# Ten-table embedding kernel on Trainium2: x in 58 loads, weights in blocks of up to 16 tiles

## The reference

```python
VOCABS = [12500, 6250, 2500, 1250, 625, 250, 1000, 500, 200, 100]
embs = [jnp.dot(x, w) for x, w in zip(xs, ws)]     # x: 1024 x vocab, w: vocab x 64, float32
emb_sum = sum(embs)
q_emb   = sum(jnp.dot(x ** 2, w ** 2) for x, w in zip(xs, ws))
fm_ans  = 0.5 * (emb_sum ** 2 - q_emb)
return jnp.concatenate([fm_ans] + embs, axis=-1)
```

## Time and profile before

| | before |
|---|---|
| median of 3 runs | 276.47 us (276.41 to 276.67) |
| the profiled execution, own time | 276.46 us |
| its span, first to last instruction | 274.7 us |
| DMA: packets, bytes, rate over the span | 15710, 113.92 MB, 415 GB/s |
| busy: PE / DVE / ACT / POOL | 78% / 82% / 82% / 42% of the span |
| x loads | 42 of 2048 KB, 9 of 1024, 11 of 512, 4 of 256 |
| weight loads | 31, of 32 to 256 KB |
| granted TensorE clock, mean | 0.988 |

### The profile page before, as it was taken

How to read it: one execution, slowest core, us unless ns; L and a number is a source line. 1 busy time by engine, 2 the same in 40 slices (tenths; PEclk the granted TensorE clock), 3 DMA queues, 4 the chain that set the end, 5 groups by cost and what they waited for, 6 DMA issues and landing times.

```text
span 274.7 us, 2715 instructions
## 1 busy us (share of the span) xinstructions
PE 213.9 (78%) x891; PEld 151.0 (55%) x892; DVE 224.1 (82%) x136; ACT 224.7 (82%) x269; POOL 114.9 (42%) x82
## 2 busy tenths in 40 slices
PE   0529889699988867878887787788788688698995
PEld 0416566476756555656654555555555465466763
DVE  2676876888798798878978978987987897999985
ACT  1649998999988788899868878877877796899994
POOL 0446757585414109267235135045045051073922
PEclk9968999999999999999999999999999999999999
DMA  7999999999999999999999999999999999999997
GB/s 263 441 402 440 410 420 417 426 421 442 416 424 426 427 420 426 421 423 428 420 424 430 420 431 428 417 424 429 420 427 431 419 423 430 410 414 416 410 398 269
DMA packets 15710, 113.92 MB, mean 415 GB/s; under 512 B 2000, under 2 KB 3280, under 8 KB 9168
## 3 DMA queue, kind: packets, MB, share of 16 engines
q1 hardware_dynamic: 11088, 106.96, 92.9%
q10 hardware_dynamic: 4608, 6.79, 6.7%
HBM read 110.85 MB, written 2.88 MB: 414 GB/s over the span
## 4 chain that ended last, share of the span: by engine, by line
DMA 63%; ACT 13%; issue 12%; PE 7%; SPq 1%; POOL 1%; ACTq 1%; DVE 0%; POOLq 0%
DMA x_ring<-in_x_dram 58%; ACT is_set L379 9%; PE sums L510 6%; DMA whole<-in_w_dram 5%; ACT turned L390 2%; SPq L327 1%; ACT whole L371 1%; POOL total L481 1%; ACT results L395 1%; ACTq L365 1%; PE sums L520 0%; ACT L371 0%; PE sums L554 0%; POOL high L468 0%; PE sums L527 0%
## 5 line engine op out<-in xcount | busy, mean ns | idle before, releaser
L604 DVE TENSOR_SCALAR_CACHE_REDUCE is_one<-x_ring 128x4096 uint8<-128x4096 f32 (+2 forms) x59 | 219.6, 3732 | 45.9 <-DMA x_ring<-in_x_dram 44.4
L379 ACT ACTIVATE is_set<-x_ring 128x2048 fp32r<-128x2048 uint32 (+2 forms) x106 | 190.1, 1796 | 32.1 <-DMA x_ring<-in_x_dram 31.6
L510 PE MATMUL sums<-is_set,low 128*128 128x512 f32 x396 | 133.1, 417 | 57.8 <-ACT is_set L379 42.8
L510 PE MATMUL sums<-is_set,high 128*128 128x512 f32 x396 | 124.9, 396 | 0.0
L510 PEld LDWEIGHTS sums<-is_set,low 128*128 128x128 f32 x396 | 68.1, 190 | 97.7 <-ACT is_set L379 43.3
L468 POOL CAST high<-whole 128x1024 fp32r<-128x1024 f32 (+5 forms) x31 | 27.1, 874 | 140.9 <-ACT whole L371 140.9
L510 PEld LDWEIGHTS sums<-is_set,high 128*128 128x128 f32 x396 | 75.5, 191 | 17.5
L470 POOL TENSOR_TENSOR low<-whole,high 128x1024 fp32r<-128x1024 f32 (+5 forms) x31 | 60.8, 1961 | 2.5
L371 ACT ACTIVATE whole<-whole 128x512 f32<-128x512 f32 (+5 forms) x31 | 16.5, 535 | 7.3 <-DMA whole<-in_w_dram 7.3
L379 ACT ACTIVATION_READ_ACCUMULATOR is_set<-x_ring 128x1 f32 x106 | 19.8, 187 | 0.0
L481 POOL TENSOR_TENSOR total<-total,turned 128x1024 f32<-128x1024 f32 x8 | 19.2, 2398 | 0.0
(11 more groups left out here) (37 smaller groups left out, 13.7 us busy)
## 6 DMA issues: line engine op xcount, KB each, us to landing
x_ring<-in_x_dram SPq DMA_DIRECT2D x42, 2048.0 KB, 21.5
x_ring<-in_x_dram SPq DMA_DIRECT2D x9, 1024.0 KB, 19.1
x_ring<-in_x_dram SPq DMA_DIRECT2D x11, 512.0 KB, 17.8
whole<-in_w_dram ACTq DMA_DIRECT2D x21, 256.0 KB, 9.7
out_dram<-results SPq DMA_DIRECT2D x9, 256.0 KB, 9.1
x_ring<-in_x_dram SPq DMA_DIRECT2D x4, 256.0 KB, 14.3
whole<-in_w_dram ACTq DMA_DIRECT2D x2, 192.0 KB, 7.1
whole<-in_w_dram ACTq DMA_DIRECT2D x4, 64.0 KB, 8.8
```

The source lines that it names most:

```text
L379: nc.scalar.activation(is_set[chunk.k % SETS][:, 0:length], in_ring(chunk.place, length).bitcast(U32), ACT.Sign, accum_out=set_counts[:, c ...
L510: last = nc.tensor.matmul(sums[:, summing(n, half), :], w, x[:, at:at + HALF], start=first, stop=False, skip_group_check=True)
L604: nc.vector.tensor_scalar(is_one[c % 2][:, to:to + length], in_ring(at, length), 1.0, None, ALU.is_equal, ALU.add, accum_out=one_counts[:, ...
```

## The change

Three things change. In `ORDER`, groups of 5 tiles (`FIVE = [2, 2, 1]`) take the place of the rests: table 3 is 5 + 5 instead of 8 + 2, the end of table 1 is 4 + 5 instead of 8 + 1, the end of table 0 is 5 + 5 instead of 8 + 2. A group of five is one load of x of 2560 KB and two counts on VectorE, of 4 tiles and of 1. In the last table two single-tile chunks share one load of 2 tiles. Together: 66 loads of x become 58 (6 of 2560 KB, 36 of 2048, 11 of 1024, 1 of 512, 4 of 256), VectorE's 59 counts become 61, 106 chunks become 108. The places in the ring move: 19 tiles, loads 0 to 5, are loaded without a wait, and load 43 starts again at the head of the ring, leaving tiles 16 to 19 of it unused for that round.

Weights are loaded in blocks: block 0 is groups 0 to 2, and after it each block is two groups, up to 16 tiles, in one of two buffers. A block whose groups belong to one table is one DMA, otherwise one per table. 15 blocks make 20 DMAs. The first two blocks (five DMAs) are issued at the start; block b is issued in the group that lies two before the first group of block b-1. `square` waits until every DMA of its block has landed. The pairs of weight parts are three instead of four.

```diff
 FULL = [2, 2, 2, 2]
+FIVE = [2, 2, 1]
...
-    (4, [[2, 2, 1]]),
+    (4, [FIVE]),
     (7, [[2, 2]]),
-    (3, [FULL, [2]]),
-    (1, [FULL] * 6 + [[1]]),
+    (3, [FIVE, FIVE]),
+    (1, [FULL] * 5 + [[2, 2], FIVE]),
     (6, [FULL]),
-    (0, [FULL] * 12 + [[2]]),
+    (0, [FULL] * 11 + [FIVE, FIVE]),
...
-WHOLES = 3
-PAIRS = 4
+BLOCK = 16
+FIRST = 3
+WHOLES = 2
+PAIRS = 3
...
-        self.whole, self.pair = g % WHOLES, g % PAIRS
+        self.pair = g % PAIRS
+        self.block, self.slot = 0 if g < FIRST else (g - FIRST) // 2 + 1, 0
...
-        elif one.table == LAST:
-            parts = [(chunk.tile, chunk.n) for chunk in chunks]
         else:
             parts = [(one.tile, sum(chunk.n for chunk in chunks))]
...
+for block in BLOCKS:
+
+    block.landed = sum(len(other.parts) for other in BLOCKS[:block.b + 1] if other.whole == block.whole)
...
-            def load_w(group):
-                if group.g >= WHOLES:
-
-                    act.wait_ge(parts_ready, group.g - WHOLES + 1)
-                at, n = group.tile * D, group.tiles
-                act.dma_start(whole[group.whole][:, 0, 0:n, :], w_dram[group.table][:, at:at + n * D]
-                              ).then_inc(w_landed[group.whole], 16)
+            def load_w(block):
+                if block.b >= WHOLES:
+
+                    act.wait_ge(parts_ready, BLOCKS[block.b - WHOLES].last + 1)
+                for table, tile, n, slot in block.parts:
+                    act.dma_start(whole[block.whole][:, 0, slot:slot + n, :],
+                                  w_dram[table][:, tile * D:(tile + n) * D]).then_inc(w_landed[block.whole], 16)
 
             def square(group):
-                act.wait_ge(w_landed[group.whole], 16 * (group.g // WHOLES + 1))
-                w = whole[group.whole][:, :, 0:group.tiles, :]
+                block = BLOCKS[group.block]
+                act.wait_ge(w_landed[block.whole], 16 * block.landed)
+                w = weights_of(group)
...
-            for group in GROUPS[:AHEAD]:
-                load_w(group)
+            for block in BLOCKS[:WHOLES]:
+                load_w(block)
...
-                        if group.g + AHEAD < NGROUPS:
-                            load_w(GROUPS[group.g + AHEAD])
+                        for block in BLOCKS[WHOLES:]:
+                            if BLOCKS[block.b - 1].first - AHEAD + 1 == group.g:
+                                load_w(block)
```

More of the change, by code:

```diff
@@ L95, in __init__ @@
         self.g, self.place, self.table, self.tile = g, place, table, tile
-        self.whole, self.pair = g % WHOLES, g % PAIRS
-        self.chunks, at = [], 0
+        self.pair = g % PAIRS
+        self.block, self.slot = 0 if g < FIRST else (g - FIRST) // 2 + 1, 0
+        self.chunks, self.sizes, at = [], sizes, 0
         for n in sizes:
@@ L145, in plan_counts @@
             parts = [(one.tile, 1), (one.tile + 1, 1)]
-        elif one.table == LAST:
-            parts = [(chunk.tile, chunk.n) for chunk in chunks]
         else:
             parts = [(one.tile, sum(chunk.n for chunk in chunks))]
+        if one.group.sizes == FIVE and one.at:
+            load = counts[-1].loads[0]
+            counts.append(Count(len(counts), [load], chunks))
+            counts[-1].at, counts[-1].length = load.at + one.at * BATCH, BATCH
+            one.place, one.load, load.count = counts[-1].at, load, counts[-1]
+            continue
+        if one.group.sizes == FIVE:
+            parts = [(one.tile, sum(FIVE))]
         length = sum(n for _, n in parts) * BATCH
@@ L159, in plan_counts @@
         counts.append(Count(len(counts), own, chunks))
+        if one.group.sizes == FIVE:
+            counts[-1].length = LOAD * BATCH
         place = own[0].at
@@ L174, in plan_counts, with __init__ @@
     return loads, counts
+class Block:
+    def __init__(self, b, groups):
+        self.b, self.whole, self.first, self.last = b, b % WHOLES, groups[0].g, groups[-1].g
+        self.parts, slot = [], 0
+        for group in groups:
+            group.slot = slot
+            if self.parts and self.parts[-1][0] == group.table:
+                self.parts[-1][2] += group.tiles
+            else:
+                self.parts.append([group.table, group.tile, group.tiles, slot])
+            slot += group.tiles
+        assert slot <= BLOCK
+BLOCKS = [Block(b, [group for group in GROUPS if group.block == b]) for b in range(GROUPS[-1].block + 1)]
+for block in BLOCKS:
+    block.landed = sum(len(other.parts) for other in BLOCKS[:block.b + 1] if other.whole == block.whole)
 LOADS, COUNTS = plan_counts()
@@ L226, in rec_kernel @@
         probe_high = sb("probe_high", [P, 1], F32R)
-        whole = [sb(f"whole{i}", [P, 2, GROUP, D], F32) for i in range(WHOLES)]
+        whole = [sb(f"whole{i}", [P, 2, BLOCK, D], F32) for i in range(WHOLES)]
         high = [sb(f"high{i}", [P, GROUP, 2 * D], F32R) for i in range(PAIRS)]
@@ L283, in upper, with weights_of @@
             return words.bitcast(BF16).rearrange("p (e h) -> p e h", h=2)[:, :, 1]
+        def weights_of(group):
+            return whole[BLOCKS[group.block].whole][:, :, group.slot:group.slot + group.tiles, :]
         def part_of(group, part):
@@ L458, in _ @@
                 g = group.g
-                w, first = whole[group.whole][:, :, 0:group.tiles, :], part_of(group, high)
+                w, first = weights_of(group), part_of(group, high)
                 pool.wait_ge(squared, g + 1)
@@ L465, in _ @@
                     nc.gpsimd.tensor_copy(pieces[:, 0, :].rearrange("p (m d) -> p m d", m=2),
-                                          whole[group.whole][:, :, group.tiles - 1, :]
+                                          w[:, :, group.tiles - 1, :]
                                           ).then_inc(pieces_ready, 1)
```

## The result

The changed kernel takes 281.96 us, the median of six runs; the kernel before took 276.44 us beside it (276.35 to 276.67, six runs). Five of the six lie between 280.56 and 282.52; the sixth ran in a slow state, at a mean TensorE clock of 0.576, took 347.17 us and is left out of the ratio. The ratio is 1.0183, 95% interval [1.0165, 1.0201]. The time went up by 5.5 us by the medians and 5.1 by the ratio, where 0.7 were forecast, and it is above the range. The profiled execution took 280.82 us, 4.4 more than that of before, with a span of 279.1 where it was 274.7.

A forecast was written before the change was run, and what follows sets the result against it. The prediction took the kernel to be bound by its 16 DMA engines. Its terms, -1.4 + 1.1 + 1.0 = +0.7 on 276.46 us, gave 277.2 us, own range 276.6 to 278.6, 8-in-10 range 275.3 to 278.8.

The forecast's parts named there:

- Term 1: DMA queues: 19 loads fewer, 171 packets per engine at 8.4 ns, save 1.4 us.
- The case of a fixed time that holds the engines: All DMAs: about 2.0 us fixed per DMA would make nineteen fewer worth 38 us; chance 0.01.
- Rival (d): Loads of x: 20 KB rows are cut, so packets aren't fewer; +0.4, 277.6 us; shares the forecast's chance of 0.48.
- Term 2: Start: joint weight waits make ScalarE late and leave DMA engines idle at 40 to 60 us; +1.1 us, bounds 0 to 2.5.
- the catching up: ScalarE, 6.5 us late near 26 us, regains 2.5 from waits it no longer has, staying 4.0 late at 53.5.
- Where the fifth weight load lands: Start: the fifth weight load lands with the fifth load of x, 14 tiles in, at 22.7 us.
- Term 3: End: the last table's tiles 16 and 17 share one load, so TensorE finishes later; +1.0 us, ends 0 and 1.3.
- sign (4): End, in the new profile: from the landing of tiles 16 and 17 to the end, 1 us more than 10.3.
- At nothing: Costs priced at zero: third pair, later parts_ready, added is_set and counts, and load 43's shorter lead, 3.3 us of store remaining.
- (a): Start: the store suffices, the fifth weight load lands near 21.5 and no DMA engine idles; 276.1 us; chance 0.24.
- (b): Start and end: the store suffices and the last table's pairs cost little, 0.4; 275.4 us; chance 0.18.
- (c): Deep starvation: store empty from 27 us on, every ScalarE delay a DMA delay; 3 us, 279.1 us; chance 0.09.

The follow-up runs named there:

- e1: The changed kernel, but each of the first five weight loads has its own semaphore: 276.81 us, ratio 1.0008 to the kernel before.
- e4: The kernel before with only the change's weight blocks and three pairs, groups and loads of x as before: 276.09 us, ratio 0.9966.
- e2: As e1, but the last table's single-tile chunks have loads of their own again: 276.77 us, ratio 0.9998.
- e8: The changed kernel with 56 idle identity matmuls on TensorE behind its second chunk: 286.37 us, ratio 1.0353.
- e3: The kernel before with only the change's groups and loads of x, weights loaded group by group, four pairs: 281.1 us, ratio 1.0155.
- e7: The changed kernel, joint waits kept, with the three five-tile loads of tables 4 and 3 cut into 4 + 1 tiles: 277.01 us, ratio 0.9999.
- e5: As e1, but with the end of table 0 as before and the last table's pairs kept: 277.28 us, ratio 1.0014.
- e6: As e5, but with single-tile loads in the last table: 276.36 us, ratio 0.9988.
- e9: The changed kernel with 24 idle identity matmuls on TensorE behind its second chunk: 280.72 us, ratio 1.0128.

## Why the prediction was wrong

**Term 1 (-1.4) was right in its count and, for the weights, in its price.** The packets are the forecast ones; the last byte of x lands 1.15 us earlier in e1, and the blocks alone, 11 x 9 = 99 packets per engine less, give 0.94 us, which is 9.5 ns each, 6.7 to 12.0 by the interval, if all of it is packets. The part of x's loads (8 x 9 = 72 packets, 0.6 us) no run shows in its time. The last byte of x lands 0.75 us earlier in e1 than in e4, which has the same weight loads, but 0.8 earlier than in e2 too, which has only four loads of x more, so single traces don't settle it. The trace's 8.4 ns and the 10.5 ns of the Trainium skill (page "DMA: Bandwidth & Descriptors", section "Measured (HBM→SBUF, 128 partitions, SWDGE, issued from GpSimd)") both lie inside. The case of a fixed time that holds the engines falls: nineteen DMAs fewer never brought a gain near 38 us. Rival (d), the cut 20 KB rows, falls with the counts: 9936 packets on q1.

**Term 2 (+1.1, bounds 0 to 2.5) failed in its size; its mechanism and its times up to 26 us were right.** It cost 4.4 us. The step that failed is the catching up: "together 2.5. It stays 4.0 us late at 53.5". By ScalarE's rows the `is_set` that ends the 9th tile was done 6.8 us later than before (33.69 for 26.88), the one that ends the 24th still 6.8 (53.71 for 46.88), and the one that ends the 28th, the next but one, 5.6 (58.93 for 53.35). First before, then after:

```profile
44.96 1.92 ACT L379 ACTIVATE is_set<-x_ring 128x2048 fp32r<-128x2048 uint32 x1
...
51.45 1.90 ACT L379 ACTIVATE is_set<-x_ring 128x2048 fp32r<-128x2048 uint32 x1
```

```profile
52.65 1.06 ACT L420 ACTIVATE is_set<-x_ring 128x1024 fp32r<-128x1024 uint32 x1
...
57.01 1.92 ACT L420 ACTIVATE is_set<-x_ring 128x2048 fp32r<-128x2048 uint32 x1
```

So the wait of 1.15 us at 48.12 did come back, as forecast, but the one of 1.06 at 20.55 did not. The prediction took ScalarE as free to use it. But ScalarE's copy waits for TensorE's transposes, they for TensorE's chunk, and the chunk for the late `is_set`: 4.6 us of path before, 5.0 now, whatever ScalarE no longer waits for. In the place of the wait for weights stands the idle time of 1.87 us. The prediction had this path nowhere: it didn't ask who waits for TensorE. In the end 0.9 of the 2.5 us were caught up: 5.6 us late at 53 stands where 4.0 was forecast. The larger error is the price: the lateness was set against a store of 2.4 to 3.0 us, and only the rest counted. From 35 to 65 us ScalarE is busy for 30.00 of 30 us, and e8 shows each later us lost in full.

A second part was missed. The prediction counted idle DMA engines only: the DMA share, from 1.02 to 0.94 over 30 us, is 2.4 us of the 4.4. The rest lies in DMA engines that are busy but slower. The queue of x, in 35 to 65 us, before and after (packets, MB, time as a share of the 16 engines):

```profile
q1 hardware_dynamic: 780, 11.47, 90.3%
```

```profile
q1 hardware_dynamic: 660, 9.75, 84.0%
```

Per MB that is 2.36 us before (0.903 x 30 / 11.47) and 2.58 after; at the old pace 9.75 MB would have taken 23.0 us and took 25.2. In e8 it is 73.2% for 8.25 MB, 2.66; in e1, with no dip, 91.5% for 11.65 MB, 2.36 again. So x's packets run some 10% longer while the store is low (2.50 in e3, whose dip is the mildest). Why they do isn't settled; no run isolates it.

**Where the fifth weight load lands** was placed rightly ("with the fifth load of x", 22.7), but for the wider lesson the text blamed the joint wait, which e4 shows to be harmless by itself. What put the landing at 22.6 instead of 18 was x's part of the change, the 20 KB rows and one load fewer (e3, e7). Either half of the mechanism, left out, removes the loss: own waits, with all five loads issued at the start (e1), or short early rows (e7).

**Term 3 (+1.0)** has nearly the right size, 0.7 to 0.9 between e5 and e6, but it isn't the only hold there. That the changed kernel's end is 1.1 us longer, as sign (4) had it, is in part luck: its chain has no DMA behind 239 us, so the end doesn't hang on the landing of the pair, and in e2 the pair's going changes nothing. **At nothing** had the ring's wrap: the landing after 12.0 was right (12.4), the DMA engines stayed busy, but the step looked only at their store. ScalarE, which waits 2.56 us for that load, stays on the path to the end. It fits that the pairs cost nothing in e1 as long as that stands (e2), and the wrap nothing as long as the pairs stand (e5). The third pair was rightly at nothing as far as shown: GpSimd waited 3.7 us once for TensorE, at 112 us, and e4, with three pairs, is faster than before.

**The rivals.** (a) and (b) fall with the dip. (c), 3 us and 279.1, was nearest; its price was too low, since it too left out the slower packets. Its condition, "the store is down to nothing from 27 us on", was met by the prediction's own figures: ScalarE 6.5 us late, and a store that lasts to 27.5. The lateness had to be carried on from there; it was compared with the store at 53.5 instead, which is that of a kernel in time.

Between the profile's 4.4 us and the median's 5.5 there is about 1 us that no trace shows. The profiled run has two more stretches at half clock, at 109 and 242 us, which the kernel before has not, and the runs' mean TensorE clocks differ (0.969 to 0.98), so more or longer stretches of the kind are a candidate. Against it: the run with the highest mean clock, 0.98, took 281.96 us. It stays open.

## What to carry to other kernels

When a change makes an engine late and the work in store covers it, follow the lateness step by step to the first moment at which the store is empty. From there on price it at its full length unless that engine has measured slack. A wait that it no longer has is slack only if nothing else on its path, here TensorE's chunk at half clock, holds it just as long. The loads of one queue, here their size and number, set when small, urgent loads in another queue land, so widen rows only where nothing urgent goes beside them; where two holds of like length sit at an end, test them together, since each alone shows nothing. Here the half of the change worth keeping is the blocks of weights with three pairs: 276.09 us, 0.34% under the kernel before.

## What the runs showed of the hardware

- Two small loads of weights (160 KB and 128 KB) issued near 10 us (9.05 and 10.62, then 9.79 and 11.26 in e3) landed at 16.2 and 20.5 beside x rows of before, and at 20.3 and 26.4 beside those with 20 KB rows, their bytes being the same.
- With the queue nearly empty, x's packets took 2.58 to 2.66 us of the 16 engines' time per MB, for 2.36 with a full one, so the rate fell by more than the idle share tells. The DMA line of the page, which shows an 8 in one slice, hid most of a 15% dip that the GB/s line shows.
- After 5.9 us without work TensorE ran at half clock: 3.76 us for eight matmuls of 512 columns, for 2.1 at full clock; the kernel before did the same after 5.27 us (3.74 us). Idle matmuls in the gap (e9) kept the clock at 1.00. The page's clock line doesn't show every slow matmul: at 14.6 to 20.1 us of the changed kernel it says 1.00, but two matmuls took 1.05 us each time, as at half clock, where 0.62 is usual.
- The same chunk runs at half clock in e4 too, from 22.4 us, and e4 is the fastest kernel here.
